# Mamba-style scan with feed-forward on one Trainium2 core: compact B with a padded band in two regions, C rows in sixteen DRAM copies, x^T issued ahead of the last C rows, and the pieces of d moved by one slot

## What is computed

```python
x = x + attn(_layernorm(x))          # below
x = x + ffn(_layernorm(x))           # two dense 512x512 products and a gate per token

def attn(x):                          # Di = 1024 channels, N = 16 states
    xn = layernorm(x) * ln_gamma + ln_beta
    x_ssm, z = split(xn @ W_in.T)
    x_ssm = silu(causal_conv4(x_ssm) + conv_b)
    xp = x_ssm @ W_xproj.T            # 33 columns: dt, B (16), C (16)
    dt = softplus(xp @ W_dt.T + b_dt) + 0.001
    A = -exp(A_log)
    # step over the 4096 tokens, for every channel and state
    dA = exp(A * dt_t); dB = (1 - dA) / (A + 1e-8) * B_t
    h = clip(dA * h + dB * x_t, -10, 10)
    y_t = sum_n(C_t * h) + D_param * x_t
    return (y * silu(z)) @ W_out.T
```

## Time and profile before

| | us |
|---|---|
| median of 3 runs (5722.37 to 5758.62) | 5735.11 |
| the profiled execution's own time | 5701.11 |
| its span | 5699.3 |
| busy in the span: PE, DVE, ACT, POOL | 4816.0, 3895.2, 3190.6, 2948.4 |
| granted TensorE clock, mean | 0.91 |

### The profile page before, as it was taken

The page is one execution under the profiler, slowest core; times in us unless marked ns, Lnnn a source line. Parts: engine busy times, 40 slices in busy tenths (PEclk is TensorE's granted clock), DMA queues, the critical chain, the costliest instruction groups (busy, mean ns, idle before and its releaser), DMA issues. The chain is left out here.

```text
span 5699.3 us, 52848 instructions
## 1 busy us (share of the span) xinstructions
PE 4816.0 (85%) x14838; PEld 2753.1 (48%) x14838; DVE 3895.2 (68%) x4219; ACT 3190.6 (56%) x5654; POOL 2948.4 (52%) x1272
## 2 busy tenths in 40 slices
PE   4878888787578898889888999999889948888888
PEld 3655555565333343334333444444434427666766
DVE  5565655556378898889888988898889934443443
ACT  2553535444467787778777887787778821111100
POOL 1211212111267797778777887888778822222221
PEclk9898888888789999999999999999999979989989
DMA  6454454554546655665566556654665551212121
GB/s 186 145 164 149 153 146 152 165 145 164 162 137 172 172 158 159 173 173 156 160 172 179 161 164 179 179 170 149 179 171 179 159 154 59 74 62 70 61 71 52
DMA packets 610685, 831.02 MB, mean 146 GB/s; under 512 B 112394, under 2 KB 317522, under 8 KB 592467
## 3 DMA queue, kind: packets, MB, share of 16 engines
q1 hardware_dynamic: 565203, 745.22, 45.4%
q10 hardware_dynamic: 45312, 83.90, 3.9%
HBM read 598.35 MB, written 267.39 MB: 152 GB/s over the span
## 5 line engine op out<-in xcount | busy, mean ns | idle before, releaser
L822 POOL TENSOR_TENSOR q<-g,cc 128x1024 f32<-128x1024 f32 x1024 | 2402.1, 2365 | 617.6 <-PE ps_y L905 483.9
L989 DVE TENSOR_TENSOR_SCAN g<-dd,carry,ps_a 128x512 f32<-128x512 f32 x2048 | 2450.5, 1260 | 386.7 <-ACT ps_a L851 246.1
L905 PE MATMUL ps_y<-q,w_s 128*128 128x512 f32 x4104 | 2221.8, 623 | 22.7 <-POOL q L822 9.8
L883 PE MATMUL ps_d<-dm,xk 99*128 99x512 f32 x2064 | 1663.6, 807 | 272.1 <-DMA xk<-xt_d 234.3
L834 ACT ACTIVATE dd<-ps_d 128x512 f32<-128x512 f32 x2064 | 1223.5, 593 | 667.9 <-PE ps_d L883 640.7
L851 ACT ACTIVATE ps_a<-dt_s,small 128x512 f32<-128x512 f32 x2051 | 1415.4, 690 | 0.0
L905 PEld LDWEIGHTS ps_y<-q,w_s 128*128 128x128 f32 x4104 | 743.3, 194 | 866.0 <-issue 451.8
L883 PEld LDWEIGHTS ps_d<-dm,xk 99*128 99x128 f32 x2064 | 399.6, 194 | 816.0 <-issue 759.7
L437 PE MATMUL ps_r_f<-xnt_hi,w_hi 128*128 128x512 f32 x1024 | 423.6, 414 | 181.3 <-ACT zs_f L353 164.7
L437 PE MATMUL ps_r_f<-xnt_hi,w_lo 128*128 128x512 f32 x1024 | 416.2, 406 | 0.0
L437 PE MATMUL ps_r_f<-xnt_lo,w_hi 128*128 128x512 f32 x1024 | 415.3, 406 | 0.0
(11 more groups left out here) (154 smaller groups left out, 5541.8 us busy)
## 6 DMA issues: line engine op xcount, KB each, us to landing
w_s<-w_d SPq DMA_DIRECT2D x129, 1088.0 KB, 5.0
xk<-xt_d SPq DMA_DIRECT2D x777, 132.0 KB
cc<-xp_d SPq DMA_DIRECT2D x68, 1024.0 KB, 14.0
xt_d<-xt_f SPq DMA_DIRECT2D x256, 256.0 KB, 2.2
dm<-bt_d SPq DMA_DIRECT2D x204, 264.0 KB
y_lo<-y_d SPq DMA_DIRECT2D x18, 2048.0 KB, 7.8
bt_d<-bt_d SPq DMA_DIRECT2D x34, 1056.0 KB, 19.6
dt_s<-dt_d SPq DMA_DIRECT2D x129, 256.0 KB, 4.2
```

What stands on the lines that cost most here:

```text
L822: pool.tensor_tensor(q[:, s % QB:s % QB + 2, :], g[:, s % GB:s % GB + 2, :], cc[:, n:n + 2, :], ALU.mult).then_inc(s_q, 1)
L883: pe.matmul(ps_d[:, parity, :], xk[:, i // HALF, i % HALF, :], dm[:, i, :, :].rearrange("p t n -> p (t n)"), start=True, stop=True).then_i ...
L905: pe.matmul(ps_y[:, m % 2, :], w[:, m % 2, n * P:(n + 1) * P], q[:, s % QB, :], start=(n == 0), stop=(n == NS - 1)).then_inc(s_n, 1)
L989: dve.tensor_tensor_scan(g[:, s % GB, :], dd[:, m % 2, n, :], ps_a[:, s % AB, :], carry[:, m, n:n + 1], ALU.add, ALU.mult).then_inc(s_g, 1)
```

## The change

1. **B.** `bt_d` keeps only 32 numbers per token. A new tensor `band_d` has two regions (even and odd chunks) of 513 padded rows for each half of the float split; its zeros are written once, in `setup` (four stores of 128x4x528 numbers and four single rows). Front's `clear_b` is gone. In the scan, `fill_band` copies 513 rows of 32 numbers from `bt_d` into the padded rows of one region, twice per chunk (DRAM to DRAM), in block 0 of the chunk before, and once ahead of the first chunk. `load_b` reads from `band_d`.
2. **C.** Front also stores the C rows of a chunk sixteen times (`c_d`), and `load_c` reads 4 rows as one run of 8 KB per partition, 8 partitions from each copy.
3. **Order.** C rows 8 to 15 (loads 2 and 3) leave the last block; they are issued in block 0 of the chunk that uses them, behind `xk`, dt, xs and x_prev, and behind them `fill_band`.
4. **Pieces.** Slot 0 makes and moves pieces 0 and 1 of the next block, slot n piece n+1, slot 15 none. `weigh_bc`, tied to piece 6, moves from slot 6 to slot 5.
5. **DVE.** `t` is made after scan 6 and the finish after scan 7; `t` has a new wait, for PE to have added the whole block before.

```diff
-BT = (BLK + 1) * NS
+BAND = (BLK + 1) * NS
+COPIES = 16
-        bt_d = nc.dram_tensor("bt_d", [2, BATCH + 1, PAD, BT], F32).ap()
+        bt_d = nc.dram_tensor("bt_d", [2, BATCH, PAD, 2 * NS], F32).ap()
+        band_d = nc.dram_tensor("band_d", [2, 2, CH + 1, BAND], F32).ap()
+        c_d = nc.dram_tensor("c_d", [COPIES, BATCH, NCH, NS * CH], F32).ap()
...
+                for e in range(2):
+                    for h in range(2):
+                        sp.dma_start(band_d[e, h, 0:1, :], zeros[0:1, :]).then_inc(s_zero, 16)
+                        sp.dma_start(band_d[e, h, 1:CH + 1, :].rearrange("(s p) n -> p s n", p=P),
+                                     bcast(zeros[:, 0:1], [(0, SUB), (1, BAND)])).then_inc(s_zero, 16)
...
-                        clear_b((ch + 1) // NCH, (ch + 1) % NCH)
                         sp.wait_ge(s_xn, ch * SUB + SUB)
...
+                        sp.dma_start(c_d[:, b, k, :].rearrange("r (n t) -> n r t", t=CH),
+                                     bcast(xp[1 + NS:NX, 0:1], [(0, COPIES), (1, CH)])).then_inc(s_xpo, 16)
...
-    BC_AT, FINISH_AT, T_AT = 6, 6, 7
+    BC_AT, T_AT, FINISH_AT = 6, 6, 7
...
+        def blocks(n):
+
+            return (0, 1) if n == 0 else (n + 1,) if n < NBLK - 1 else ()
...
+                def fill_band(c, b, k):
+
+                    for h in range(2):
+                        sp.dma_start(band_d[c % 2, h, :, 0:2 * NS], bt_d[h, b, bass.ds(k * CH, CH + 1), :],
+                                     allow_slow_non_contiguous=True).then_inc(s_band, 16)
...
                 def load_c(b, k, i):
-                    row = xp_d[b, 1 + NS + 4 * i:5 + NS + 4 * i, bass.ds(k * CH + 1, CH)]
-                    sp.dma_start(cc[:, 4 * i:4 * i + 4, :], row.partition_broadcast(P)).then_inc(s_cc[i], 16)
+                    src = c_d[:, b, k, 4 * i * CH:(4 * i + 4) * CH]
+                    sp.dma_start(cc[:, 4 * i:4 * i + 4, :].rearrange("p n t -> p (n t)"),
+                                 bass.AP(tensor=src.tensor, offset=src.offset,
+                                         ap=[tuple(src.ap[0]), (0, P // COPIES), (1, 4 * CH)])).then_inc(s_cc[i], 16)
...
                             load_dt_xs(*at(m + 1))
+                            if m == 0:
+                                if ch > 0:
+                                    for i in range(2, 4):
+                                        sp.wait_ge(s_q, pairs(ch, 4 * i + 4 - NS))
+                                        load_c(b, k, i)
+                                    sp.wait_ge(s_dm[PIECES - 1], 48 * ch)
+                                fill_band(ch + 1, b1, k1)
...
                             if m == MD - 1:
-                                for i in range(2, 4):
-                                    sp.wait_ge(s_q, pairs(ch, NS * m + 4 * i + 4))
-                                    load_c(b1, k1, i)
                                 load_b_ahead(b1, k1)
...
-                            move_d(ch, m + 1, n)
+                            for i in blocks(n):
+                                move_d(ch, m + 1, i)
...
                 def self_term(ch, m):
 
+                    dve.wait_ge(s_n, summed(ch, NS * m))
```

More of the change, by code:

```diff
@@ L68, in build, with setup @@
             within = sb("within", [P, MD, NS], c=early)
-            setup(nc, sb, sem, t_in, ident, ones, minus_half, margin, within, xs_d, xp_d, xt_d, bt_d, w_d)
-            front(nc, sb, sem, t_in, ident, ones, minus_half, margin, within, clips, xs_d, dt_d, zs_d, xp_d, xt_d, bt_d)
-        scan(nc, sb, sem, ident, clips, xs_d, dt_d, zs_d, xp_d, xt_d, bt_d, w_d, y_d)
+            setup(nc, sb, sem, t_in, ident, ones, minus_half, margin, within, xs_d, xp_d, xt_d, bt_d, band_d, w_d)
+            front(nc, sb, sem, t_in, ident, ones, minus_half, margin, within, clips, xs_d, dt_d, zs_d, xp_d, xt_d, bt_d, c_d)
+        scan(nc, sb, sem, ident, clips, xs_d, dt_d, zs_d, xp_d, xt_d, bt_d, band_d, c_d, w_d, y_d)
         ffn(nc, sb, sem, t_in, ident, minus_half, y_d, out)
-def setup(nc, sb, sem, t_in, ident, ones, minus_half, margin, within, xs_d, xp_d, xt_d, bt_d, w_d):
+def setup(nc, sb, sem, t_in, ident, ones, minus_half, margin, within, xs_d, xp_d, xt_d, bt_d, band_d, w_d):
     with ExitStack() as c:
-        zeros = sb("zeros", [P, 16], c=c)
+        zeros = sb("zeros", [P, BAND], c=c)
         a_log = sb("a_log", [P, MD, NS], c=c)
@@ L165, in _, with front @@
                     dve.sem_inc(s_w, 1)
-def front(nc, sb, sem, t_in, ident, ones, minus_half, margin, within, clips, xs_d, dt_d, zs_d, xp_d, xt_d, bt_d):
+def front(nc, sb, sem, t_in, ident, ones, minus_half, margin, within, clips, xs_d, dt_d, zs_d, xp_d, xt_d, bt_d, c_d):
     HALO = TAPS - 1
@@ L219, in _ @@
             def _(sp):
[L220 to L224, removed]
                 def store_turned(ch, b, k, i):
@@ L599, in _, with scan @@
                 dve.wait_ge(s_fl, 3)
-def scan(nc, sb, sem, ident, clips, xs_d, dt_d, zs_d, xp_d, xt_d, bt_d, w_d, y_d):
+def scan(nc, sb, sem, ident, clips, xs_d, dt_d, zs_d, xp_d, xt_d, bt_d, band_d, c_d, w_d, y_d):
     STEPS = MD * NS
@@ L635, in scan @@
         s_pass, s_init = S("pass"), S("init")
-        s_sm, s_bcl, s_ba = S("small"), S("bcl"), S("ba")
+        s_sm, s_band, s_bcl, s_ba = S("small"), S("band"), S("bcl"), S("ba")
         s_dm = [S(f"dm{i}") for i in range(PIECES)]
@@ L710, in store_y @@
                     sp.dma_start(y_d[b, m, :, bass.ts(k, CH)], zs[:, m % 2, :]).then_inc(s_yo[m % 2], 16)
+                fill_band(0, 0, 0)
                 for h in range(2):
                     load_x(0, 0, 0, h, 0)
-                    load_b(0, 0, 2 * h)
-                    load_b(0, 0, 2 * h + 1)
+                sp.wait_ge(s_band, 32)
+                for i in range(PIECES):
+                    load_b(0, i)
                 sp.dma_start(small[:, :, :], w_d[:, :, W_BIG:W_COLS].rearrange("m p s -> p m s"),
@@ L746, in _ @@
                             if m == MD - 2:
+                                sp.wait_ge(s_band, 32 * (ch + 2))
                                 sp.wait_ge(s_dps, ch * STEPS + NBLK * (m + 1) + EACH)
-                                load_b(b1, k1, 0)
+                                load_b(ch + 1, 0)
                             if m == MD - 1:
```

58 lines of the change are left out of this document (27 added, 31 removed).

## The result

The changed kernel takes 5477.06 us (median of 4 runs, 5469.65 to 5484.81) beside 5732.52 for the kernel before (4 runs): ratio 0.9548, 95% interval 0.9512 to 0.9583. The forecast was 5506, range 5370 to 5700, with faster at 0.84. The profiled execution of the changed kernel took 5481.68 us, that of before 5701.11, so the difference that the traces explain is 219.4; 229 was forecast for it. The forecast of 5506 stands 34 above its own figure for a profiled execution, since before's profiled execution was that much faster than before's median; the changed kernel's is 4.6 slower than its median. The total fits better than its terms do.

What follows compares the result with a forecast made beforehand. Bounds: front by x behind the clears, steady blocks by the POOL and PE loop, chunk boundaries by a full DMA queue. Front -153, setup +8, boundaries -78, first chunk -6 make -229: 5472 profiled, 5506 as median, range 5370 to 5700.

Steps and rivals of the forecast that it cites:

- Front: Front's fifteen later chunks: without the clears ahead of x, each takes 80.0 us instead of 90.2, -153 us in all.
- Setup: Setup stage: four stores of zeros ahead of the w stores cost +8 us (0 to 15).
- C load: Scan's queue: a load of C rows costs 3 us instead of 6.8, each DMA engine reading its own copy.
- Band: Scan's queue: the two DRAM-to-DRAM band copies of 513 runs of 128 B cost 5 us together.
- Boundaries: Passing between chunks: loss falls from 21.1 to 15.9 us a chunk, including a new 7.5 us wait at block 1; -78 us.
- first chunk: First chunk's scan: band ahead of `dm` +5, four cheaper C loads -15, new queue +4; -6 us.
- Pieces and t: Steady scan blocks: the new order of pieces and `t` costs +0.09 us a block, 0.7 a chunk.
- 1: Scan's queue costs more than it gives: C loads stay at 6.8 us, band costs 16; 5872 us, chance 0.06.
- 2: Scan's queue: C loads stay at 6.8 us with band at 5; 5694 us, no change that can be told, chance 0.10.
- 3: Steady blocks: DVE's wait for the last piece of d was the bound, 106 us more gained; 5400 us, chance 0.12.
- 4: Start of block 1: no new wait for x^T, 112 us more gained; 5394 us, chance 0.15.
- 5: Front gains only 5 us a chunk, PE at half clock; 5584 us, chance 0.10.

Runs made afterwards that it cites:

- before_x_first: Kernel before, with front's load of x issued ahead of the two clears of the padded B, which stay: 5549.51 us, ratio 0.9659.
- c_last_block: Changed kernel with C loads 2 and 3 moved from block 0 back to the last block, ahead of x^T's second half: 5481.91 us, ratio 0.9549.
- pieces_undone: Changed kernel with one piece of d in each slot again and the old order of B*C, `t` and finish: 5448.17 us, ratio 0.9491.
- c_2k: Changed kernel reading C rows from the old place in runs of 2 KB, sixteen copies still stored: 5549.16 us, ratio 0.9667.
- last_row: Changed kernel with `b_ahead` loaded as 128 runs of 64 B from a small tensor of last columns, not 2048 single numbers: 5414.12 us, ratio 0.9419.
- c_padded: Changed kernel with the sixteen copies of C 520 KiB apart in place of 512: 5445.14 us, ratio 0.9504.

## Why the prediction was right, and where its steps were not

*Front, -153 (75 to 225).* Right in mechanism and size: chunks 1 to 15 gave 170.1, the first chunk lost 3.3. before_x_first shows the cause alone. Chunk 0's 80.0 was a fair sample only by luck: that chunk takes 72.8 to 83.3 in the profiles of the other kernels. From the first to the last of a chunk's 16 dt products on PE it is 10.3 to 19.4 us by the granted clock, and the period goes with it.

*Setup, +8.* 4.4 in the trace. Not in the sum were 4.8 us between front and the first scan. The traces point at the copies of C: from the end of front's last dt product to the first scan it is 54.8 and 54.5 us with the kernel before's scan, 59.2 to 60.9 in the seven that read sixteen copies, 56.3 to 56.8 in the four that read one. The band copies ahead of `dm`, in all of the last eleven, may be the rest; that was not tried.

*C load, 3 us.* This step failed. I argued that a C load would cost as w's does because each engine reads its own copy. It takes 4.65; one copy takes 2.45. The reason given had the wrong sign: the form of one run of 8 KB a partition made the gain, and the copies gave back about half of it. That is 4 x 1.65 us more in the queue a chunk, not all of it on the path.

*Band, 5 us.* Mis-sized: 2.3 for both; moved away it gives 1.7. The Trainium skill's rule on the number of engines ("DMA: Bandwidth & Descriptors", on why a DMA increments its semaphore by 16) agrees with the trace as far as it shows: each band copy is recorded with one early event and nine landings. The 7 us made from it, with the price of single numbers, were three times too much.

*Boundaries, -78, and first chunk, -6.* -43 and -2.6. The base was already too high: 21.1 us of loss a chunk has the longer first chunk in it, and chunks 1 to 15 alone lose 187.05 - 166.8 = 20.2. Then two terms were off in opposite ways:
- Block 0 was to lose 3.5, with 1 more for PE at half clock behind the waits, and loses 28.98 - 20.98 = 8.0. This is the larger error, and it is one of sampling. The wait of the earlier trace rows was read in chunk 4, whose block 0 takes 43.4 us, the longest of the fifteen. Its landing moved forward by 17.5 us, more than any of the fifteen waits, and this was taken off a loss of 19.0 that is a mean. In the mean of the fifteen, block 0 loses 38.92 - 20.85 = 18.1 and piece 8 waits 11.6. With that wait gone 6.5 is left, where the prediction left 1.5. To it come 1.1 for B*C, which waits 2.5 in place of 1.45 (the prediction had 2 for it), and 0.7 for the first half of x^T, which was 1.7 late before and is 2.4 late now: 8.3, of which 8.0 is seen. Part of the 6.5 is that PE runs slow for a while: it is busy 23.64 us in block 0 of chunk 4 for the products that take 20.83 in a steady block, granted 0.88 in the mean (half of 2.4 GHz for a stretch of it):

```profile
2097.20:2118.20 21.00, 20.83 (x54) 9.25 (x53) 20.13 (x19) 18.46 (x37) 18.80 (x9) 1.00 0.45 142
...
2164.70:2193.50 28.80, 23.64 (x53) 10.45 (x52) 20.72 (x18) 18.52 (x37) 19.90 (x10) 0.88 0.81 197
```

- The new wait at the start of block 1 exists, but is 34.9 us in 14 waits, 2.3 a chunk, not 7.5, though the two C loads ahead of it cost 9.3 and not 6. A longer block 0 lets the queue catch up, and the band is cheap. The block loses 3.7. The last block loses 4.6, not 3.2; PE's "issue" wait there is 2.9 each in place of 1.7.

Moving the last C loads behind x^T was worth nothing that can be told in the scan (c_last_block): what it takes off block 0, 4.2, comes back in block 1 and the last. The 13.6 us that these two loads were to take off piece 8's wait are more than its mean.

*Pieces and t, +0.7 a chunk.* The steady block is near: 20.98 beside 20.94. With the earlier due time of x^T and B*C the order costs 1.8 a chunk (pieces_undone); the prediction had put some of that into blocks 0 and 7.

*After the scan.* No term. -15.9, of which c_last_block shows 8.8 for the order of the C loads; the likely reason for the rest is their cheaper form.

Put together for chunks 1 to 15, from the runs: C form -4.3 (c_2k to changed), pieces +1.8, order of C loads -0.1, which is -2.6 of the -2.9 seen. The two figures agree within the noise of 1. The band costs up to 1.7 besides, and what would make up for it is open.

*The rivals.* 1 and 2 had C at 6.8: that is the old form's price, in the new kernel too (6.7 at 156 GB/s), and the new form's is 4.65. 3 (DVE's wait was the bound) is refuted by pieces_undone. 4 (no wait at block 1): there is one, but 2.3 is nearer to none than to 7.5. 5 (front gives 5 a chunk) is refuted. Of the signs of being right, front's held (DVE waits 3.1 a chunk for x, the periods are 79.4); C at over 300 GB/s and the split of PE's wait did not. So the forecast was right in its sign, its mechanism in front and its range. Its closeness in the total owes something to errors that cancel: the scan gave 38 less than forecast, front's later chunks 17 and the stage behind the scans 16 more. Front's 17 is no larger than what the granted clock moves between executions.

## What to carry to other kernels

Take a wait and the loss that it is to explain from the same places: over all fifteen boundaries, not one of them. In a full queue, price every transfer up to the next due one, and then up to the one after: a load moved back is not gone, and only making it cheaper helped here. Look at what a due load stands behind: here it waited for two slow copies that it did not need (90 to 79 us a chunk for one line moved). Before copying data so that engines don't meet in DRAM, measure the single copy in long runs: here it was nearly twice as fast.

## What was not expected of the hardware

- A broadcast read of 1 MB in 8 KB runs takes 2.45 us from one copy and 4.5 to 4.65 from sixteen, whether these are 32, 512 or 520 KiB apart (packets of 309 and 566 to 571 ns in the median). In last_row, with sixteen copies, two landings are 3.55 apart though its packets take 566 ns as well; the packets are the steadier measure.
- A load of 2048 single numbers holds up SP itself: at the place shown the three issues behind it take 8.18 us, behind a load of 128 runs of 64 B 1.25.
- The same stretch of front, from the first to the last of a chunk's 16 dt products with 24 matmuls between them, takes from 10.3 to 19.4 us by the clock granted. The last chunk's stretch in the changed kernel, and in before_x_first:

```profile
1339.40:1349.60 10.20, 10.20 (x40) 5.06 (x40) 8.92 (x14) 10.07 (x18) 5.08 (x4) 1.00 0.85 221
```

```profile
1326.60:1342.80 16.20, 16.20 (x40) 7.91 (x40) 7.70 (x13) 10.90 (x17) 5.01 (x4) 0.61 0.38 130
```

The work is the same 40 matmuls, without a gap in either. Just ahead of it PE was busy for 5.50 of 9.4 us (clock 1.00) in the first and 6.69 of 10.6 (0.87) in the second; why one stretch gets 2.4 GHz and the other mostly 1.2 is open. Such differences move the whole kernel by up to 1%, from one variant to the next and between executions of the same one (c_padded's four).
